# Swapping the order in which the next unit's queries and keys are made in two many-head attention stages

## The reference, cut to what matters

```
x = x + attn0(layernorm(x))                 # single head, causal
x = x + cross_attn0(layernorm(x), ctx)      # 16 heads of 16, keys and values from ctx
x = x + block_ffn0(layernorm(x))            # 4 of 16 hidden blocks kept per token
x = x + attn1(layernorm(x))                 # 16 heads, q, k, v from x; adds its own input again
x = x + local_cross_attn1(layernorm(x), ctx)# 16 heads, rotary, masked by token ids
x = x + moe1(layernorm(x))                  # 2 of 8 experts per token, and a shared expert
```

```
q, k, v = y @ Wq.T + bq, c @ Wk.T + bk, c @ Wv.T + bv     # y: normed x; c: ctx (cross_attn0) or y (attn1)
p = softmax(q_h @ k_h.T / scale)  for each of 16 heads    # cross_attn0 also adds a mask
out = concat_h(p_h @ v_h)
```

## Time and profile before

| | |
|---|---|
| median of 3 timed runs | 784.07 us (783.26 to 785.36) |
| the profiled execution | 783.83 us, of which the span in the trace is 782.0 us |
| TensorE clock granted | 0.999 of full speed |
| TensorE matmul / weight load busy | 742.7 us (95%) / 607.4 us (78%) |
| VectorE, ScalarE, GpSimd busy | 540.1 us (69%), 422.9 us (54%), 333.2 us (43%) |

### The profile page before, as it was taken

How to read it: one execution, slowest core, us unless ns; L and a number is a source line. 1 busy time by engine, 2 the same in 40 slices (tenths; PEclk the granted TensorE clock), 3 DMA queues, 4 the chain that set the end, 5 groups by cost and what they waited for, 6 DMA issues and landing times.

```text
span 782.0 us, 16960 instructions
## 1 busy us (share of the span) xinstructions
PE 742.7 (95%) x5956; PEld 607.4 (78%) x5956; DVE 540.1 (69%) x1449; ACT 422.9 (54%) x1252; POOL 333.2 (43%) x461
## 2 busy tenths in 40 slices
PE   8999999999899999999999999999999988999996
PEld 7887777776688888877777777877777767888885
DVE  4666787878654455357677767788899988766655
ACT  3445676777522222347777766777665675433320
POOL 2332334443323212432223326666678745725540
PEclk9999999999999999999999999999999999999999
DMA  8903243220355556600000003000000001235528
GB/s 310 374 3 95 74 119 89 76 76 2 98 163 158 146 165 174 145 1 1 2 1 2 2 1 123 15 15 15 15 15 29 28 30 48 87 112 163 163 97 322
DMA packets 67042, 69.46 MB, mean 89 GB/s; under 512 B 22448, under 2 KB 57648, under 8 KB 65936
## 3 DMA queue, kind: packets, MB, share of 16 engines
q1 hardware_dynamic: 63552, 59.03, 24.7%
q0 software_dynamic: 3408, 9.34, 3.6%
HBM read 38.96 MB, written 29.40 MB: 87 GB/s over the span
## 4 chain that ended last, share of the span: by engine, by line
PE 61%; DVE 17%; POOL 7%; issue 7%; ACT 4%; DMA 3%; SPq 1%; POOLq 0%; DVEq 0%
PE pj L375 8%; PE pj L368 8%; PE pj L462 7%; PE ov L537 7%; PE sc L451 6%; PE sc L524 6%; DVE mx L1009 5%; POOL routed_y L1788 5%; PE pj L362 4%; PE ov L473 4%; DVE pT L1016 3%; PE sc L669 2%; PE sc L446 2%; ACT pr L1518 2%; PE ov L375 2%
## 5 line engine op out<-in xcount | busy, mean ns | idle before, releaser
L1518 ACT ACTIVATE pr<-sc,mx 128x128 f32<-128x128 f32 x768 | 217.5, 395 | 83.1 <-DVE mx L1009 81.1
L1009 DVE TENSOR_REDUCE mx<-sc 128x4 f32<-128x512 f32 x192 | 126.2, 683 | 36.2 <-PE sc L451 34.4
L462 PE MATMUL pj<-idn,pr 128*128 128x128 f32 x768 | 121.4, 282 | 12.7 <-DVE pT L1016 4.5
L462 PEld LDWEIGHTS pj<-idn,pr 128*128 128x128 f32 x768 | 84.0, 141 | 51.9 <-issue 25.0
L1016 DVE COPY pT<-pj 128x512 f32<-128x512 f32 x128 | 87.1, 686 | 31.8 <-PE pj L462 31.5
L1706 POOL TENSOR_SCALAR ve<-mv 128x2 f32<-128x2 f32 x40 | 13.7, 343 | 172.9 <-DVE mv L938 172.4
L1538 ACT ACTIVATE hT<-sc,vecs 128x256 f32<-128x256 f32 x64 | 30.4, 474 | 89.0 <-PE sc L524 89.0
L537 PE MATMUL ov<-W,hT 128*128 128x256 f32 x256 | 61.4, 383 | 2.4 <-DVE hT L1095 2.4
L524 PE MATMUL sc<-xnT,W 128*128 128x256 f32 x256 | 60.5, 380 | 0.0
L451 PE MATMUL sc<-kM,qT 32*128 32x256 f32 x768 | 55.0, 399 | 4.4 <-ACT pr L1518 4.0
L1501 ACT ACTIVATE pT<-pj 128x512 f32<-128x512 f32 (+1 forms) x72 | 42.1, 586 | 28.6 <-PE pj L462 28.3
(11 more groups left out here) (228 smaller groups left out, 1512.6 us busy)
## 6 DMA issues: line engine op xcount, KB each, us to landing
sorted_x<-more_xT SPq DMA_DIRECT2D x15, 1152.0 KB, 7.2
kM<-sorted_x SPq DMA_DIRECT2D x39, 129.0 KB, 2.1
cT<-in_ctxT SPq DMA_DIRECT2D x16, 256.0 KB, 3.4
pr<-kept_at SPq DMA_DIRECT2D x32, 128.0 KB, 3.2
pT<-kept_at SPq DMA_DIRECT2D x32, 128.0 KB, 3.2
W<-in_w SPq DMA_DIRECT2D x2, 1024.0 KB, 13.7
cT<-in_ctx SPq DMA_DIRECT2D x8, 256.0 KB, 3.7
W<-in_w_gu SPq DMA_DIRECT2D x1, 2048.0 KB, 8.2
```

What stands on the lines that cost most here:

```text
L462: last = tr(bank[b][:, i * S:(i + 1) * S], pr[n % 4][:, i, :], idn[:])
L1009: v.tensor_reduce(mx[n % 4][:], four(b), AX.X, ALU.max, negate=True).then_inc(mx_done, 1)
L1518: last = a(pr[n % 4][:, i, :], bank[b][:, i * S:(i + 1) * S], ACT.Exp, bias=mx[n % 4][:, i:i + 1])
```

## The change

In stages 1 and 3 the two projections change places: the next unit's queries are made in `part0` and its keys in `part1`, on TensorE and on ScalarE. `query3` gets the wait for `xnT` that `key3` had to itself (which keeps it). `masked_keys` on GpSimd stays in `part1` and so is not moved in that engine's order. The pairs are units 7 to 14 (which prepare units 8 to 15) and units 23 to 30 (which prepare 24 to 31).

```diff
             def query3(W):
                 b, n = begin("pj", "q", W)
                 pe.wait_ge(drained[b], n - 1)
+                pe.wait_ge(*emptied("xT", W))
                 across(b, Wqkv, xnT[W % 3], 0)
...
 # TensorE, part0
                 elif f == 1:
-                    key1(U + 1)
+                    query1(U + 1)
...
                 elif f == 3:
-                    key3(U + 1)
+                    query3(U + 1)
...
 # TensorE, part1
                 if f == 1:
-                    query1(U + 1)
+                    key1(U + 1)
                 elif f == 3:
-                    query3(U + 1)
+                    key3(U + 1)
...
 # ScalarE, part0
                 if f in (1, 3):
-                    keys(U + 1, "k", U + 1)
+                    queries(U + 1, f // 2)
...
 # ScalarE, part1
                 if f in (1, 3):
-                    queries(U + 1, f // 2)
+                    keys(U + 1, "k", U + 1)
```

## The result

| | before | changed |
|---|---|---|
| timed beside each other (11 runs each) | 783.32 us (781.23 to 786.15) | 779.85 us (779.01 to 780.13) |
| ratio | | 0.9947, interval 0.9935 to 0.996 |
| profiled execution / span | 783.83 / 782.0 us | 779.97 / 778.2 us |

A forecast was written before the change was run, and what follows sets the result against it. TensorE, 95% busy, was taken to bound the kernel, with small gaps from ScalarE's latency behind part1's projection. Terms -1.4 (stage 1) - 1.75 (stage 3) + 0.1 (unit 7) = -3.05 us gave 780.9 us, range 779.8 to 783.4.

The forecast's parts named there:

- Two terms of the sum: Stages 1 and 3: shorter copy behind part1's projection gives 1.4 and 1.75 us; the sum had no term outside the units.
- Place and mechanism: Part1, stages 1 and 3: ScalarE's copy delays TensorE's next step; the key copy frees bank 0.23, `exps(U,3)` 0.25 us sooner.
- The size of the term: Copy behind part1's projection: 0.23 us a unit in units 9 to 14, 0.25 us in units 24 to 30.
- Unit 7: First unit of the change: queries now come first and must wait for `xnT`, 0.1 us lost.
- Unit 8: ScalarE is the late one there; 0.25 us more ahead and 0.25 less behind give 0.
- Unit 30: Last of the seven stage 3 units counted at 0.25 us gain each, 1.75 us in all.
- Part0's copy is covered: Part0: ScalarE's work ends 0.25 us later, hidden by its idle before part1's copy, which falls from 0.58 to 0.33 us.
- Late keys cost nothing: `masked_keys` on GpSimd starts some 2.7 us later and nobody waits; 2.5 us to spare in unit 7, 7.5 in steady units.
- The collision in stage 3: `masked_keys` runs over VectorE's layer norm, which takes 1.15 us instead of 0.73, hidden with 0.08 us left.
- The rival that lived on it: Rival 2: only one stage gives; a stage 3 layer norm delayed by GpSimd leaves 782.0 us. Chance 0.23.
- The wait of the scores 0.22 instead of 0.47: Stage 3, second half: TensorE's idle ahead of the scores, behind `exps(U,3)`, falls from 0.47 to 0.22 us.
- The forecast of the time: Whole kernel: -3.05 us, 780.9 us; rival 1, both stages give their gain, 779.9 to 781.7 us, chance 0.62.

The follow-up runs named there:

- one activation, order of before: Kernel before, with the queries copied by one ScalarE activation instead of two (part of the bias left out): 785.54 us, ratio 0.9971 to before.
- the second comparison: Changed kernel run again without an edit, against the kernel before on one chip: 779.42 us against 783.78, ratio 0.994.
- the changed kernel with doubled waits: Changed kernel plus 8 doubled, always satisfied TensorE waits in stage 0 (`query0`), against the kernel before: 785.88 us against 789.02, ratio 0.9971.
- one kernel in the changed order: Changed kernel with VectorE copying the keys in stage 3 and no `kM_done` waits ahead of the copy: 782.9 us, ratio 0.992 to before.
- the kernel that had them in stage 3: Kernel before with only the new wait of `query3`, 8 satisfied wait instructions on TensorE: 788.36 us against 789.02, ratio 1.0.

## Why the prediction was right or wrong, point by point

- **The steps that failed.** Two terms of the sum. The gain of the copy was put at 0.23 and 0.25 us a unit, as if the key copy started at the moment at which the query copy had; the runs showed 0.18 us, since it starts 0.06 us later. And all that lies outside the changed units was put at nothing: 1.2 us of the two first traces' difference is the gap from the last scatter to the read of what it wrote. The sum of the units came to -2.2 us where I had -3.05, while the medians fell by 3.5 us.
- **Place and mechanism: right.** The copy behind part1's projection held the bank and `exps(U,3)`, and its length is what counts (one activation, order of before: -0.15 us a unit).
- **The size of the term: too large.** The prediction had 0.23 us a unit in stage 1 (0.84 - 0.61) and 0.25 us in stage 3 (0.73 - 0.48). Measured: 0.18 in both stages. The key copy takes 0.50 us to the next activation in its new place instead of the 0.48 read in its old one, and it starts 0.06 us later behind its projection, since `keys` has a second wait. I had called the wait added on TensorE free and had not looked at the one that came along on ScalarE. 0.25 - 0.02 - 0.06 is 0.17; in stage 1, where the end of the copy counts, 0.84 - 0.60 - 0.06 is 0.18. Without that wait the units are 0.24 to 0.25 us shorter than before (16.91 and 17.79 us), close to the forecast.
- **Unit 7: 0.17 us lost instead of 0.1. Unit 8: 0.10 gained instead of 0. Unit 30: 0.08 gained instead of 0.25.** Units 9 to 14 and 24 to 29 gave 0.18 to 0.20 us each.
- **Part0's copy is covered: right.** ScalarE's idle fell from 0.58 to 0.40 us in both stages, not to 0.33, for the same 0.06 us.
- **Late keys cost nothing: right.** No first scores wait for GpSimd. `masked_keys` starts 7.91 us after its unit's milestone instead of 5.15, 2.76 us later where 2.7 were forecast.
- **The collision in stage 3: it happens, on the other side.** I expected the layer norm at 1.15 us. In units 25 to 29 it kept its 0.73 us and GpSimd paid, 2.43 instead of 2.17 us; only in unit 24 it took 0.98. The rival that lived on it fell by this.
- **"The wait of the scores 0.22 instead of 0.47": wrong.** I took TensorE's readiness as fixed, though it stood behind the same copy.
- **The forecast of the time: near by luck.** 780.9 us were forecast and 779.85 measured, but the units' part was 0.85 us too large and a term that belongs to no edit made up for it. The medians differ by 3.5 us and, in the second comparison, by 4.4 us, because runs of before reach up to 786 or 787 us and those of the changed kernel stay within 1.4 us. The fastest runs of either are closer to the units: 781.23 against 779.01, 2.2 us, and 781.46 against 778.82, 2.6 us. On the third chip the changed kernel with doubled waits has 0.9971 (2.3 us by the ratio, 3.1 us between the medians), within an interval that takes in the units' 2.2 us.
- **Open:** why the changed orders did not show the long gap on the first chip. The traces tie it to a code packet beside the last scatter and to the clock behind it; what times that packet isn't shown, and one kernel in the changed order met it on the third chip.

## What to carry to other kernels

When an engine idles until a matmul group ends and then holds up the next one, put the shorter of two copies behind it, or give the copy to an engine that is idle there; here the total busy time of the copies stayed the same, and only their place counted. Measure the gain as the length of one repeated unit, since it repeats to 0.01 us where the kernel's time scatters by several us, and compare the rest of the program apart. When a step is moved, bring all of its waits into the sum, and expect a wait on the chain to keep its length when both of its ends hang on what was shortened.

## What the runs showed of the hardware that was not expected

- A second, long satisfied semaphore wait ahead of a ScalarE activation that waits for a matmul cost 0.06 to 0.07 us on the chain, in each repeated unit of both stages. Eight satisfied waits on TensorE changed no repeated unit by more than 0.01 us (unit 30 took 19.86 us instead of 19.77 in the kernel that had them in stage 3).
- VectorE's layer norm and GpSimd's key masking at the same time: in stage 4 VectorE paid (0.73 to 1.15 us), in unit 24 too (0.98 us), and in units 25 to 29 GpSimd did, with one of its four instructions at 0.83 instead of 0.55 us and VectorE's at 0.40 as alone. The layer norm starts 0.13 us (stage 4) and 0.28 us (unit 24) behind the start of an instruction of GpSimd where VectorE paid, and 0.37 us behind where GpSimd paid; that this decides it is not shown. This is the summary of GpSimd's line in unit 27 (duration in ns, least, median, most), and under it the same for VectorE's:

```profile
L1732 POOL TENSOR_SCALAR kM<-kraw,vecs x4: 548/553/828, 398.2 to 400.1; 128x256 f32<-128x256 f32 x4
```

```profile
L944 DVE TENSOR_SCALAR xw<-X,mv,rstd x2: 404/406/408, 399.2 to 399.5; 128x256 f32<-128x256 f32 x2
```

- The last indirect scatter landed 2.4 to 2.5 us after its issue in four traces and 3.6 and 4.3 us after it in two (the other eight give no landing); in all 14 its last write came at 2.0 to 2.2 us, or at 3.15 to 3.83 us in the four in which a packet of instruction code started 1.5 to 1.6 us behind its issue.
- TensorE idle for 2.62, 2.98 or 3.78 us near the end was followed by the lower clock (0.70 granted over 768 to 772 us in one of these traces), idle for 2.69 us once without it; the stretch behind it took 1.6 to 1.7 us longer with it.
